# Expert routing in a macaron kernel: picks from unscaled gate products, gate products ahead of the scatters, two groups, running sums for the ranks

## Reference

```
x = x + 0.5 * moe(layernorm(x), w_gate, W1, b1, W2, b2)     # 8 experts, top 2
x = x + ssm(layernorm(x), ...)
x = x + 0.5 * moe(layernorm(x), w_gate, W1, b1, W2, b2)     # the same weights
x = x + 0.5 * gated(x); x = x + global(layernorm(x)); x = x + 0.5 * gated(x)

def moe(x, w_gate, W1, b1, W2, b2):                          # tokens x 128
    gate = softmax(x @ w_gate.T)
    scores, idx = top_k(gate, 2)
    y = gelu(x @ W1[e] + b1[e]) @ W2[e] + b2[e]              # W1: 128 x 512, W2: 512 x 128
    return sum over the 2 chosen e of scores * y
```

## Time and profile before

| what | value |
|---|---|
| median of 3 runs | 2209.62 us (2207.27 to 2210.42) |
| profiled execution, its own time | 2207.21 us |
| span of the profiled execution | 2205.4 us |
| TensorE, VectorE, ScalarE, GpSimd busy | 84%, 71%, 63%, 58% of the span |
| mean granted TensorE clock | 0.924 |

### The profile page before, as it was taken

The page is one execution under the profiler, slowest core; times in us unless marked ns, Lnnn a source line. Parts: engine busy times, 40 slices in busy tenths (PEclk is TensorE's granted clock), DMA queues, the critical chain, the costliest instruction groups (busy, mean ns, idle before and its releaser), DMA issues. The chain is left out here.

```text
span 2205.4 us, 52050 instructions
## 1 busy us (share of the span) xinstructions
PE 1849.2 (84%) x16960; PEld 1410.0 (64%) x16961; DVE 1575.7 (71%) x2848; ACT 1392.0 (63%) x3948; POOL 1286.6 (58%) x1099
## 2 busy tenths in 40 slices
PE   4269956626996599999999999675999999999996
PEld 4158832415884377777777776342777777777774
DVE  4658858554885588878788886243788888788872
ACT  5135533212554488788878887364787888878873
POOL 4354410246441688878788785101887878788771
PEclk9989969658997799999999999787999999999998
DMA  6212140022214111111110110000111011111111
GB/s 204 67 60 64 41 122 0 22 74 65 61 44 128 58 28 26 24 24 26 26 28 20 26 25 16 4 0 5 31 26 26 20 28 26 23 27 23 22 23 39
DMA packets 87309, 88.28 MB, mean 40 GB/s; under 512 B 13978, under 2 KB 65863, under 8 KB 87016
## 3 DMA queue, kind: packets, MB, share of 16 engines
q1 hardware_dynamic: 77288, 68.09, 12.3%
q0 software_dynamic: 8704, 17.85, 2.4%
q10 hardware_dynamic: 1152, 0.25, 0.1%
HBM read 35.60 MB, written 22.22 MB: 26 GB/s over the span
## 5 line engine op out<-in xcount | busy, mean ns | idle before, releaser
L2040 POOL TENSOR_TENSOR mac_probs<-mac_probs,mac_prec 128x512 f32<-128x512 f32 x256 | 265.5, 1043 | 199.5 <-DVE mac_prec L1855 198.6
L1716 ACT ACTIVATE mac_probs<-banks,mac_nmax 128x128 f32<-128x128 f32 x1024 | 359.6, 386 | 0.0
L2020 POOL TENSOR_TENSOR route_pool<-route_pool 128x1024 f32<-128x1024 f32 x128 | 303.5, 2371 | 35.7 <-issue 13.1
L1812 DVE TENSOR_TENSOR route_pool<-banks,tables 128x1024 f32<-128x1024 f32 x256 | 300.7, 1214 | 33.2 <-ACT route_pool L1676 27.8
L1846 DVE TENSOR_REDUCE mac_nmax<-banks 128x4 f32<-128x512 f32 x256 | 164.8, 686 | 126.2 <-PE banks L1544 126.2
L2031 POOL TENSOR_TENSOR mac_qkn<-route_pool,mac_rc 128x1024 f32<-128x1024 f32 x128 | 243.9, 1906 | 15.8 <-issue 7.6
L854 POOL DMA_INDIRECT x_sorted<-route_pool,route_index x128 | 124.5, 973 | 216.3 <-DVE route_index L666 122.0
L862 POOL DMA_INDIRECT y_tokens<-moe_bench,moe_goal x144 | 141.0, 979 | 173.0 <-DVE moe_bench L805 123.7
L1716 ACT ACTIVATION_READ_ACCUMULATOR mac_probs<-banks,mac_nmax 128x1 f32 x1024 | 231.8, 226 | 0.0
L54 PE MATMUL banks<-wqkv_h,mac_hh 128*128 128x512 f32 x384 | 179.2, 467 | 27.4 <-POOL mac_hl L1995 22.4
L388 PE MATMUL banks<-w,moe_gh 128*128 x576 | 159.6, 354 | 46.9 <-issue 30.9
(11 more groups left out here) (315 smaller groups left out, 5086.9 us busy)
## 6 DMA issues: line engine op xcount, KB each, us to landing
mac_v_even<-mac_v SPq DMA_DIRECT2D x224, 128.0 KB, 2.2
moe_xs<-x_sorted SPq DMA_DIRECT2D x144, 72.0 KB
route_pool<-y_tokens SPq DMA_DIRECT2D x16, 512.0 KB, 7.2
y_tokens<-moe_bench,moe_goal POOLq DMA_INDIRECT x144, 2.3
moe_bench<-in_L_attn_x SPq DMA_DIRECT2D x8, 256.0 KB, 5.2
route_pool<-in_L_ffn_W SPq DMA_DIRECT2D x4, 512.0 KB, 6.8
x_sorted<-route_pool,route_index POOLq DMA_INDIRECT x128
b<-in_b_flat SPq DMA_DIRECT2D x1, 2048.0 KB
```

The source lines that it names most:

```text
L1716: e = act.activation(probs[:, r, p, :], m.ps[:, S + r, p * P:(p + 1) * P], ACT.Exp, bias=nmax[:, r, p:p + 1], accum_out=psum[:, r, p:p + 1])
L1812: turn = dve.tensor_tensor(turned[:, i, :, :].rearrange("q k (h s j) -> q k h s j", s=2, j=DH // 2), q[:, :, :, ::-1, :] if i else q, tabl ...
L2020: pool.tensor_tensor(sums[:], turned[:, 0, :, :], turned[:, 1, :, :], ALU.add).then_inc(added, 1)
L2040: pool.tensor_tensor(probs[:, r, :, :], probs[:, r, :, :], prec[:, r, :].unsqueeze(2).to_broadcast([P, HP, P]), ALU.mult).then_inc(shared[ ...
```

## The change

The two experts of a token are picked from the gate products as TensorE leaves them in PSUM; since `rstd` is positive, the order of the eight numbers stays. The scaling by `rstd` comes once for all groups, late (`scale_gaps`), ahead of the softmax weights. There are two groups of four sequences instead of three groups. GpSimd begins the first stream only when the gate products of all eight sequences are made. `select` adds four additions that make running sums over the tiles of a group (`before`, with a pad of zeros ahead), and `ranks` needs three products instead of 2n. The orders on TensorE, VectorE and ScalarE are rewritten; in the second call `turn` uses six banks and the gate products of all sequences are made before sequences 2 to 7 are transposed.

```
-    TURNS, LB, PB, CB, BACK = 4, (4, 7), (5, 6), 6, (7, 0)
+    TURN, SB, CB, BACK = (0, 1, 2, 3, 5, 6), (4, 7), 6, (7, 0)
-    GROUPS = [(0, 1), (1, NH_SEQ), (NH_SEQ, NB)]
+    SCALED = [(0, 1), (1, NH_SEQ), (NH_SEQ, NB)]
+    MOST = NH_SEQ * TT
+    AT = MOST * NE
+    PAD = MOST // 2
+    strides = lambda n: [1 << j for j in range((n - 1).bit_length())]
...
             def ranks(i):
-                pe.matmul(m.ps[:, PB[i % len(PB)], AT[i]:AT[i] + n * NE], m.low_bf[:], flat(0, n), start=True, stop=False)
-                for t in range(1, n):
-                    pe.matmul(m.ps[:, PB[i % len(PB)], AT[i] + t * NE:AT[i] + n * NE], m.ones_bf[:], flat(0, n - t), start=False, stop=t == n - 1)
-                for t in range(n):
-                    mm = pe.matmul(m.ps[:, PB[i % len(PB)], AT[i] + n * NE:AT[i] + (n + 1) * NE], m.ones_bf[:], chosen[:, t, :], start=t == 0,
-                                   stop=t == n - 1)
-                mm.then_inc(ranked, 1)
+                pe.matmul(m.ps[:, SB[i], AT:to], m.low_bf[:], flat(chosen, PAD), start=True, stop=False)
+                pe.matmul(m.ps[:, SB[i], AT:to], m.ones_bf[:], flat(sums, PAD - 1), start=False, stop=True)
+                pe.matmul(m.ps[:, SB[i], to:to + NE], m.ones_bf[:], sums[:, PAD + n - 1, :], start=True, stop=True).then_inc(ranked, 1)
...
# TensorE
             turn(0)
+            if first:
+                for b in range(1, NB):
+                    turn(b)
+                    score(b - 1)
+                    if b == NB - 2:
+                        pe.wait_ge(primed, START + 1)
+                        ranks(0)
+                score(NB - 1)
+            else:
+                for b in range(NH_SEQ):
+                    score(b)
+                turn(1)
+                for b in range(NH_SEQ, NB):
+                    score(b)
+                for b in range(2, len(TURN)):
+                    turn(b)
+                ranks(0)
+                turn(NB - 2)
             ranks(1)
+            if not first:
+                turn(NB - 1)
...
# ScalarE
             scales(0)
+            if not first:
+                double(0)
             for b in range(1, NH_SEQ):
                 keep(b)
                 deviations(b)
             scales(1)
+            if first:
+                for b in range(NH_SEQ, NB):
+                    keep(b)
+                double(0)
+            else:
+                for b in range(1, NH_SEQ):
+                    double(b)
             for b in range(NH_SEQ, NB):
                 deviations(b)
-            scales(HALF)
+            scales(2)
             if first:
+                for b in range(1, NH_SEQ):
+                    double(b)
                 weight_uppers()
-            weigh()
             for b in range(NH_SEQ, NB):
                 double(b)
+            weigh()
...
# VectorE, gates and select
-                dve.wait_ge(deviated, START + i + 1)
-                step(dve.tensor_tensor(z, m.ps[:, LB[i % len(LB)], lo * TT * NE:hi * TT * NE].rearrange("p (t e) -> p t e", e=NE),
-                                       rstd[:, by_tile(lo, hi)].unsqueeze(2).to_broadcast([P, n, NE]), ALU.mult))
-                step(dve.tensor_reduce(peak[:, :n], z, AX.X, ALU.max))
-                dve.tensor_tensor(z, z, peak[:, :n].unsqueeze(2).to_broadcast([P, n, NE]), ALU.subtract).then_inc(peeled, 1)
+                step(dve.tensor_reduce(peak[:], raw, AX.X, ALU.max))
+                dve.tensor_tensor(z, raw, peak[:].unsqueeze(2).to_broadcast([P, MOST, NE]), ALU.subtract).then_inc(peeled, 1)
...
-                dve.tensor_tensor(chosen[:, :n, :], won[:, 0], won[:, 1], ALU.add).then_inc(selected, 1)
+                step(dve.tensor_tensor(chosen[:, PAD:PAD + n, :], won[:, 0], won[:, 1], ALU.add))
+                part = chosen
+                for j, s in enumerate(strides(n)):
+                    part, last = before[:, j % 2, :, :], part
+                    sm = dve.tensor_tensor(part[:, PAD:PAD + n, :], last[:, PAD:PAD + n, :], last[:, PAD - s:PAD - s + n, :], ALU.add)
+                    if s != strides(n)[-1]:
+                        step(sm)
+                sm.then_inc(selected, 1)
+
+            def scale_gaps():
+
+                dve.wait_ge(deviated, START + len(SCALED))
+                dve.tensor_tensor(gap[:], gap[:], rstd[:].unsqueeze(2).to_broadcast([P, NB * TT, NE]), ALU.mult).then_inc(scaled, 1)
...
# VectorE, the order
             gates(0)
             select(0)
             norms(0)
-            means(3)
             positions(0)
             gates(1)
             select(1)
-            norms(1)
+            if first:
+                for b in range(NH_SEQ, NB):
+                    means(b)
+            else:
+                for b in range(1, NH_SEQ):
+                    means(b)
             positions(1)
-            norms(2)
-            norms(3)
-            for b in range(NH_SEQ, NB):
-                means(b)
-            gates(HALF)
-            select(HALF)
-            positions(HALF)
+            for b in range(1, NH_SEQ):
+                norms(b)
             if first:
                 dve.wait_ge(rest_in, START + 32)
+            else:
+                for b in range(NH_SEQ, NB):
+                    means(b)
             tables()
...
             for b in range(NH_SEQ, NB):
                 norms(b)
+            scale_gaps()
             shares()
...
# GpSimd
-            for i, (lo, hi) in enumerate(GROUPS[:HALF]):
-                pool.wait_ge(indexed, START + i + 1)
-                pool.wait_ge(marked, START + 1)
-                for n in range(lo, hi):
-                    pool.wait_ge(normed, START + n + 1)
-                    for t in range(TT):
-                        send_x(n, 0, t)
-                    pool.wait_ge(doubled, START + n + 1)
-                    for t in range(TT):
-                        send_x(n, 1, t)
+            pool.wait_ge(scored, START + NB)
+            pool.wait_ge(indexed, START + 1)
+            pool.wait_ge(marked, START + 1)
+            for n in range(NH_SEQ):
+                pool.wait_ge(normed, START + n + 1)
+                for t in range(TT):
+                    send_x(n, 0, t)
+                pool.wait_ge(doubled, START + n + 1)
+                for t in range(TT):
+                    send_x(n, 1, t)
             pool.wait_ge(scattered[0], 16 * TOP * TT * NH_SEQ)
-            pool.wait_ge(indexed, START + len(GROUPS))
-            pool.wait_ge(doubled, START + NB)
+            pool.wait_ge(indexed, START + HALVES)
             pool.wait_ge(marked, START + 2)
...
+                pool.wait_ge(doubled, START + n + 1)
                 for k in range(TOP):
```

More of the change, by code:

```diff
@@ L478, in weigh @@
             def weigh():
[L480 removed]
+                act.wait_ge(scaled, START + 1)
                 act.activation(weight[:], gap[:], ACT.Exp).then_inc(exped, 1)
@@ L645, in norms @@
             def norms(b):
+                dve.wait_ge(deviated, START + [lo <= b < hi for lo, hi in SCALED].index(True) + 1)
                 for t in range(TT):
@@ L733, in _ @@
                 dve.memset(m.mean_of[:], 1.0 / P).then_inc(blanked, 1)
+            step(dve.memset(chosen[:, :PAD, :], 0.0), False)
+            step(dve.memset(before[:, :, :PAD, :], 0.0), False)
             step(dve.memset(route.owner[:, :GROUP], 0), False)
@@ L736, in _ @@
             means(0)
-            means(1)
             if first:
+                means(1)
                 dve.wait_ge(order_in, START + 32)
@@ L747, in _ @@
             marks(0)
-            means(2)
+            if first:
+                means(2)
+                means(3)
             gates(0)
```

82 lines of the change are left out of this document (25 added, 57 removed).

## The result

| | time, us | ratio to before, 95% interval |
|---|---|---|
| before, median of 5 runs | 2209.62 (2207.27 to 2211.2) | |
| changed, median of 5 runs | 2198.47 (2196.25 to 2203.55) | 0.9954 [0.994, 0.9969] |
| predicted | 2188.6 (2180 to 2201) | |

By the medians the kernel is 11.15 us faster where 21 were forecast. The ratio and its interval are estimated over all the runs and are not the quotient of the two medians (0.9950); by the ratio the gain is 10.2 us. The sign is right and the time lies in the range; the size is half. The profiled execution took 2203.55 us and is the slowest of the five; its span, 2201.8, is only 3.6 us shorter than the span before.

The account below looks back on a forecast made before the run. It took late TensorE signals beside GpSimd's scatters to delay the path to the loop and the loop itself. Starts 13.4 and 4.3 us sooner plus 2 x 1.6 gave 21: 2186.2 profiled, 2188.6 median, range 2180 to 2201.

Parts of the forecast that it names:

- The scatters' start: First stream, both calls: GpSimd starts later, at 31.1 in the first call and 429.7 instead of 418.88 in the second.
- the signal of `ranks(1)`: Routing, second group: with three products, TensorE's signal comes about 1 us late, covered by `means` of 3.2 and 2.4 us.
- The work that was behind it: `tables`, `weight_lowers`, `marks(1)`, `norms(4..7)` move under the first stream, end 8 and 14 us before TensorE starts, cost nothing.
- the forecast's 13.4 us: First call: TensorE begins the loop at 78.4 instead of 91.77, 13.4 us sooner.
- The rule that was weighed: Two-port VectorE instructions lock GpSimd out: 28 `norms` would lengthen the first stream by up to 7.6 us, gain 13; not adopted.
- SyncE reads its rows and starts loading: After the first stream: loads start at 74.6 and 474.2, TensorE at 78.4 and 478.0, 13.4 and 4.3 us sooner.
- The loop: Expert loop: the second stream starts 4 us before TensorE, so 3 us less scattering gives 1.6 us more per call.
- The sum: Both calls: 13.4 + 4.3 + 2 x 1.6 = 21 us gained.
- The more small instructions: TensorE's signals beside scatters come later the more products just issued: 4.4 us after 24, 13.3 and 14.7 after 32.
- Signals still late: Rival, 0.16: the three products' signal waits for a stream pause and 3.7 us more; gain 11, 2198.6 us.
- The loop follows GpSimd: Rival, 0.13: the loop gains what the second stream's earlier start gains, 28.6 us in all; 2181 us.
- Slower: Rival, 0.05: the signal is held 13.3 us or more whatever its size; at 14.7, 2.8 us slower, 2212.4.

Follow-up runs that it names:

- e1: Changed kernel, with VectorE in the first call waiting for all 32 first-stream scatters to land before `weight_lowers`: 2159.66 us, 1.0125 to the kernel before, prompt chip.
- e6: Changed kernel, with ScalarE copying raw expert weights into PSUM and `weight_lowers` subtracting from there: 2190.34 us, 0.993 to the kernel before, late chip.
- wait alone: Kernel before, with GpSimd waiting for all eight sequences' gate products before its first scatter: 1.0008 on a late chip, 1.013 on a prompt one.
- e7: Kernel before, with running sums, three products in `ranks` and subtractions read from PSUM: 2204.72 us, 0.9995; again 2205.1, 1.0005; both late chips.
- e10: Kernel before, with GpSimd's wait for all gate products, running sums and three products in `ranks`: 2165.89 us, 1.0153, prompt chip.
- e2: Changed kernel, with GpSimd's second stream held in both calls until the first 16 loads land: 2184.98 us, 1.0236; again 2182.06, 1.0246; prompt chips.
- e3: Changed kernel, with the old 2n products in `ranks` instead of three: 2158.02 us, 1.0105; again 2154.81, 1.0112 and 2158.95, 1.013; prompt chips.
- e11: Changed kernel, with the old 2n products in `ranks` in its second call only: 2154.04 us, 1.0105 to the kernel before, prompt chip.
- e4: Kernel before, with running sums in `select` and three products in `ranks` alone, three groups kept: 2137.62 us, 1.0011, prompt chip.

## Why the prediction was half right

**The scatters' start and the signal of `ranks(1)`: right.** First scatters at 30.69 and, from each call's start, 20.6 (forecast 21.4); pauses of 0.12 and 1.16 us beyond the usual 0.30; `positions(1)` 2.6 us or less behind its products.

**The step that failed: "The work that was behind it ... They cost nothing."** `weight_lowers` was put under the stream at no price, and it makes one scatter 9.4 us longer; the stream's end is 9.7 us later than forecast. e1 and e6 show it from two sides: the subtractions away from the stream, and the subtractions in place with one operand from PSUM. Of the forecast's 13.4 us it leaves 3.6; with it gone e6 starts its loop at 78.92, 12.8 us before the kernel before on that chip. Of these 9.7 us, e6 gets back 6.6 by the medians and 5.0 by the means.

The rule that was weighed was the right page, looked at for the wrong instructions. I tested it on `norms`, one input from SBUF, and those cost little: beside `norms(4..7)`, from 66.28 to 70.48, the scatters take 0.97 to 1.01 us. The Trainium skill, SBUF, "SBUF: two separate sides", names beside the two-port modes the VectorE instruction with two inputs from SBUF, this one only against a GpSimd instruction that reads SBUF (a scatter takes its rows and row numbers from there), and says that whichever starts first gets the port pair that the two engines share for the whole instruction. The traces agree for the eight large subtractions (10.40 us with two SBUF inputs, 0.97 with one), and in part for smaller ones: scatters beside a product of 0.94 us in `tables`, the 0.41 us of `scale_gaps` and a product of 0.68 us in `shares` took 1.54, 1.22 and 1.38 us, while others beside such instructions of `tables` kept 0.97 to 1.00.

**Second: "SyncE reads its rows and starts loading ... TensorE begins at 78.4 and 478.0."** The second call's first load was on time (66.0 us after the call's start, forecast 65.9), but 3.8 us from there to TensorE became 8.6. In the first call the scatters had only just begun and it was 4.0. From the first to the 16th load the changed kernel takes 25.1 to 28.2 us in the second call of its three late traces and 12.5 to 14.3 in the first. Two things have to meet for that. The loads must lie beside scatters: in the kernel before, whose second call issues them ahead of its second stream, it is 8.8 us on a late chip too, and in the changed kernel the loads come mostly 0.5 to 0.8 us apart again from 492.39 on, while GpSimd scatters nothing (490.2 to 503.14). And the chip must be late: in e1, on a prompt one, GpSimd's second stream starts at 452.79, SyncE's loads at 453.08, and it is 8.8 us. Whether holding the stream would pay on a late chip was not seen: both holds ran on prompt ones.

**The loop: 1.6 us a call forecast, not seen clear of the spread.** From TensorE's start to the 14th tile the late traces of the kernel before took 62.1, 61.5, 58.6 and 61.5 us (mean 60.9), those of the changed kernel 61.8, 61.8, 58.3, 58.9, 55.1 and 56.1 (58.7), 2.3 less on average. It does not last: to the end of the last result's scatter it is 199.9 to 203.0 us before (mean 201.1) and 197.4 to 202.4 after (200.3), 0.8 less, where traces of one kernel differ by up to 5. The third stretch of scatters began 28.4 to 29.1 us after TensorE in the first call and 28.7 to 32.2 in the second, where 29 to 31 was to show the forecast right.

**The sum.** The first loop starts 3.6 us sooner. The second, from its call's start, takes 72.7 on average (74.55, 71.52, 72.14) against 74.5 (74.00, 74.99), 1.8 sooner. With 2 x 0.8 for the whole loops that is 7 us; the three comparisons of medians measured 11.2, 9.4 and 8.0. The 1 to 4 us between aren't located; they are less than the 4 to 10 us by which runs of one kernel on one chip differ here. Against the forecast's 20.9 the traces have 9.8 less at the first start, 2.5 less at the second and 1.6 less in the loops.

**"The more small instructions": not refuted, not shown, and too narrow.** Signals late by 13.0 to 16.1 (kernel before, two late chips) and 10.4, 8.4 (wait alone) after 32 products, and at most 2.6 after three, speak for the number. The number alone, in one place, was never tried on a late chip, so this stays open. And other handings over are late without a number: 11.4 us for one transpose in e7. On late chips neither of two parts gains alone: the wait gives 1.0008, the running sums (with the subtractions from PSUM) 0.9995 and 1.0005, the whole 0.9951 to 0.9964. Whether these two together are enough, or the two groups and the rewritten orders are needed, was not seen: both parts together (e10) ran on a prompt chip only.

**The rivals.** *Signals still late* had named 2198.6 us, and 2198.47 was measured. That is chance: its mechanism, `norms(1)` held up by the signal, did not happen, and the time was lost at `weight_lowers` and SyncE's loads instead. *The loop follows GpSimd* does not hold on late chips, where 197 to 201 us pass from the start of the 33rd scatter to that of the last result's in the kernel before and 201 to 210 in the changed one, so the earlier scatters are mostly lost. It fits the prompt ones: 182 to 186 us in 22 calls of eleven traces, and with e2's second streams 11.1 and 10.9 us later than e3's the time is 27 us longer. *Slower* came true on prompt chips, by a mechanism that I had not written down: with no late signal to remove, the later first stream (its first scatter at 30.7 in e11, at 20.3 in e4) is only lost.

**What to do with it.** e6 beats both kernels on the late chip where it ran, the kernel before by 16.0 us and the changed one by 6.6, though the fastest runs of the changed kernel (2188.8) reach its own (2188.26 to 2191.91). On prompt chips nothing tried beat the kernel before; the early stream with subtractions from PSUM (e7) was not seen there.

## What to carry to other kernels

A forecast from one trace is a forecast for that chip: when a wait fits no recorded instruction, look at the kernel on a second chip before rebuilding an order around it. When work moves under GpSimd's scatters, go through VectorE's instructions by their operands: here those with two large inputs from SBUF stopped the scatters for as long as they ran, and one operand in PSUM freed them. And what is moved under a stream must be priced even where the mover has time to spare, since it is the stream that pays.

## What the runs showed of the hardware

Chips differ in how other engines fare beside GpSimd's scatters. In the three sets of runs on late chips (that of the earlier trace rows among them) VectorE and ScalarE see TensorE's work up to 16 us late, SyncE issues one load in 1.7 to 1.9 us beside them in the changed kernel's second call and in 0.8 to 1.0 in its first, and TensorE takes 50 to 57 us for the loop's first 13 tiles. On the prompt ones `positions` of the last group follows its products within 2.6 us, SyncE issues every 0.6 us and the 13 tiles take 26 to 28. The scatters themselves are alike on both, 0.97 us and a step of 1.27. The same kernel takes 2205 to 2210 us on one and 2130 to 2135 on the other, and the same change gives 0.995 to 0.996 on one and, one `ranks` aside, 1.0105 on the other.
